# Looping over the batches and loading each adjacency unit in two halves

## The chip, the cores and the metric

The kernel runs on one core of a Trainium2 chip. The metric is the device time of one execution in microseconds. A second number, the span, is the time from the first to the last instruction in a profiled execution.

## The reference

```python
# x: (8, 2048, 64), adj (called W): (8, 2048, 2048), U: (2048, 16), w_scale: scalar, all float32
Ws = 0.5 * (W + jnp.swapaxes(W, -1, -2))
A = jax.nn.sigmoid(U @ U.T)
K = Ws * A[None, :, :]
deg = jnp.maximum(K.sum(axis=-1), EPS)
d = jax.lax.rsqrt(deg)
K = K * d[:, :, None] * d[:, None, :]
y = w_scale * jnp.einsum('bnm,bmc->bnc', K, x)
out = _layernorm(x + y, axis=-1)
```

For each of 8 batches a 2048 x 2048 matrix of 16 MB is read, made symmetric, multiplied by a gate that is the same for all batches, normalized by its row sums on both sides and applied to x. A layer norm over the 64 channels follows.

## The kernel before

Each batch's matrix is cut into 4 x 4 units of 512 x 512, 1 MB each, held in SBUF as `K[(i, j)]`, a tile of 128 partitions by 4 chunks by 512. There is one buffer for each of the 16 units, so the units of the next batch are loaded into the buffers that this batch frees. The symmetric sum and the row sums are made in ten steps (`STEPS`, pairs i >= j), of four rows each (128 matrix rows): rows 0 to 39 of a batch. The steps are (0,0), (1,0), (1,1), (2,0), (3,0), (2,1), (3,1), (3,2), (2,2), (3,3).

For one row of step (i, j) PE transposes pieces of K[(j, i)] into the PSUM ring `tw` (four banks, L394 called by `transpose_adjacency`), DVE adds them to K[(i, j)] (`add_row`, L663), then multiplies by the gate and sums the row (`gate_product`, L674, which signals `lower_done`). PE transposes the result back into the PSUM pair `kt` (L394, called by `transpose_rows`) and ACT copies it to K[(j, i)] (`upper_row`, L556, `upper_done`). When a group of rows has its degrees, POOL makes d and DVE makes z = d * x (L694). PE then forms the products z^T K (L434), in eight pairs of units (`PAIRS`): (0,0) with (0,1), (0,2) with (0,3), (1,0) with (1,1), (1,2) with (1,3), (2,0) with (2,1), (3,0) with (3,1), (2,2) with (2,3), (3,2) with (3,3). Each pair has four chunks, each of two products, and the last one signals `prod_done`. The layer norm of a batch runs on DVE, POOL and ACT two batches later.

All orders are written out by hand. A table gives for each piece of work the row at which it stands; `PRODUCT_ROWS` places the 32 product chunks of a batch at rows 29 to 65, where 40 and more mean rows of the next batch. `steps(b, lags)` issues the 40 rows of batch b with what is left of the one or two batches before; each engine has its own. The batches are unrolled by Python, so every wait is against a constant.

SP issues the loads (`load_unit`, L250). `load_pair(b, q)` waits for `prod_done` of pair q in the batch before and then loads both units of the pair, (0,1) ahead of (0,0) in pair 0, otherwise the first named first. Behind pair 5 stands the store of batch b - 2. Each unit has its own semaphore `loaded`, for which DVE (row 0 of a step, for K[(i, j)]) and PE (row 0, for K[(j, i)]) wait.

Of the kernel before, what the change touches and what calls it, by code (L numbers as in the profile page):

```python
# [13 lines left out]
P = 128  # L14
G = 4
H = P // 2
UW = G * P
# [16 lines left out]
PAIRS = PRODUCT_ORDER  # L34
# [78 lines left out]
def bass_graph_resnorm_kernel(nc, x, adj, u, w_scale, out):  # L113
# [6 lines left out]
    with ExitStack() as ctx:  # L120
# [95 lines left out]
        tw_done, sum_done, lower_done = sem("tw_done"), sem("sum_done"), sem("lower_done")  # L216
        kt_done, upper_done = sem("kt_done"), sem("upper_done")
        deg_summed, deg_ready, d_ready, z_ready = sem("deg_summed"), sem("deg_ready"), sem("d_ready"), sem("z_ready")
        prod_done, y_copied, yt_done = sem("prod_done"), sem("y_copied"), sem("yt_done")
        f_ready, y_scaled, h_ready = sem("f_ready"), sem("y_scaled"), sem("h_ready")  # L220
# [25 lines left out]
        def _(sp):  # L246
            def load_unit(b, n):
                i, j = n
                src = adj[b, i * UW:(i + 1) * UW, j * UW:(j + 1) * UW].rearrange("(g p) m -> p g m", p=P)
                sp.dma_start(K[n][:, :, :], src).then_inc(loaded[n], 16)  # L250

            sp.dma_start(u_sb, u.rearrange("(g p n) r -> p g n r", p=P, n=G)).then_inc(h_moved, 16)
            for k, n in enumerate(FIRST_LOADS):
                if k == X_AFTER:
                    sp.dma_start(xt[:, :, :], rows_of(x, 0)).then_inc(x_loaded, 16)
                if n in ((3, 2), (2, 3)):
                    sp.wait_ge(ut_done, 8)
                if n in ((2, 2), (3, 3)):
                    sp.wait_ge(uu_done, NL)
                load_unit(0, n)  # L260
            def load_pair(b, q):
                sp.wait_ge(prod_done, b * NQ + (q + 1 - NQ))
                for n in (LOADS[0:2] if q == 0 else PAIRS[q]):
                    load_unit(b, n)

# [4 lines left out]
            for q in range(NQ):  # L270
                load_pair(1, q)
            for b in range(2, B):
                for q in range(NQ):
# [13 lines left out]
        def _(pool):  # L287
# [67 lines left out]
            steps(1, 2)  # L355
            for b in range(2, B):
                steps(b, 3)
# [22 lines left out]
        def _(pe):  # L380
            def bank_free(b, g, first):
# [4 lines left out]
                elif not first:  # L386
                    last = max(n for n in range(NL) if tw_bank[n] == tw_bank[g])
                    pe.wait_ge(sum_done, b * NL + (last + 1 - NL))

            def transpose_halves(dst, at, blocks):  # L390

# [6 lines left out]
            def transpose_adjacency(b, s, r, first):  # L398

                i, j = STEPS[s]  # L400
                if r == 0:
                    pe.wait_ge(loaded[(j, i)], b * 16 + 16)
                bank_free(b, s * G + r + 1, first)
                for row in (r, r + 1):
                    g = s * G + row
# [4 lines left out]
            def transpose_rows(b, s, r, first):  # L410
# [5 lines left out]
                if not first or g:  # L416
                    pe.wait_ge(upper_done, b * NU + g)
                for row in range(r, min(r + 2, upper_rows(s))):
                    transpose_halves([kt[:, h, :] for h in range(2)], HALF_ROW * (row % 2),
# [3 lines left out]
            def product(b, q, c, first):  # L423
# [8 lines left out]
                for n, m in PAIRS[q]:  # L432
                    at = (m % 2) * C
                    t = pe.matmul(yp[at:at + C, m // 2, :], z[:, n * G + c, :], K[(n, m)][:, c, :],  # L434
                                  start=(q == first_unit[m] and c == 0), stop=(q == last_unit[m] and c == G - 1))
                if c == G - 1:
                    t.then_inc(prod_done, 1)
# [78 lines left out]
            steps(1, 2)  # L516
            for b in range(2, B):
                steps(b, 3)
# [20 lines left out]
        def _(act):  # L539
# [77 lines left out]
            steps(1, 2)  # L617
            for b in range(2, B):
                steps(b, 3)
# [25 lines left out]
        def _(dve):  # L645
# [10 lines left out]
            def add_row(b, g):  # L656
# [3 lines left out]
                if r == 0:  # L660
                    dve.wait_ge(loaded[STEPS[s]], b * 16 + 16)
                dve.wait_ge(tw_done, b * NL + (g // 2 * 2 + 2))
# [160 lines left out]
            steps(1, 2)  # L823
            for b in range(2, B):
                steps(b, 3)
# [46 lines left out]
```

## Time and profile before

| what | value |
|---|---|
| median of 3 runs | 486.77 us |
| lowest and highest | 483.96 and 487.22 us |
| the profiled execution | 483.64 us |
| its span | 481.9 us |
| mean granted clock of PE, share of full speed | 0.988 |
| HBM traffic over the span | 296 GB/s |

The profiled execution's time is 1.7 us more than its span. The engines are called PE (TensorE), DVE (VectorE), ACT (ScalarE), POOL (GpSimd) and SP (SyncE). PEld is PE's weight load, which overlaps the matmuls. Times of rows are in microseconds from the start of the span.

### The profile page before, as it was taken

The numbers are of one execution on the slowest core, as the hardware profiler recorded it, in microseconds if no ns is written. First come the engines' busy times: TensorE is split into PE (matmuls) and PEld (weight loads), VectorE is DVE, ScalarE is ACT, GpSimd is POOL, SyncE is SP. The second block draws the span as 40 slices with busy tenths as digits, with TensorE's granted clock in tenths as the row PEclk, the third lists the DMA queues.
The fourth block names the chain that finished last, engine by engine and source line by source line (L and its number), as shares of the span: only waits on it lengthen the run. The fifth ranks groups of instructions, "written<-read, shape, count | busy, mean of one in ns | idle before, by whom it ended". The sixth has DMA issues, their size and how long they took to land.

```text
span 481.9 us, 13213 instructions
## 1 busy us (share of the span) xinstructions
PE 440.4 (91%) x5318; PEld 232.3 (48%) x5318; DVE 416.6 (86%) x1154; ACT 209.4 (43%) x655; POOL 113.8 (24%) x133
## 2 busy tenths in 40 slices
PE   7887999899989999889998999899998899999893
PEld 6555544454445534554444543465445544455351
DVE  6888867899889989999879997899889998899745
ACT  3887424453245433544254442454434542554320
POOL 0000010023410334012520243103340125203343
PEclk9999999999999999999998999989999999999998
DMA  8999799959999699968999699997999889994011
GB/s 289 387 312 391 283 372 377 310 180 365 356 365 309 251 361 368 344 253 296 361 357 300 221 350 364 325 287 266 371 354 329 284 298 357 367 296 169 1 45 44
DMA packets 101420, 143.58 MB, mean 298 GB/s; under 512 B 35824, under 2 KB 35824, under 8 KB 101360
## 3 DMA queue, kind: packets, MB, share of 16 engines
q1 hardware_dynamic: 86496, 139.01, 82.0%
q10 hardware_dynamic: 14864, 3.74, 3.7%
q8 instruction: 42, 0.69, 0.6%
q14 instruction: 18, 0.15, 0.1%
HBM read 138.54 MB, written 4.19 MB: 296 GB/s over the span
## 4 chain that ended last, share of the span: by engine, by line
PE 56%; DMA 21%; DVE 13%; ACT 4%; issue 3%; SPq 2%; POOL 0%; POOLq 0%; DVEq 0%
PE yp L434 33%; DMA k<-in_adj_dram 20%; PE tw L394 9%; PE kt L394 9%; DVE k L663 5%; DVE k L674 5%; PE yp L532 3%; ACT k L556 2%; SPq L250 2%; ACT gate L543 2%; PE yp L467 1%; DVE deg L684 1%; DMA h<-in_L_gnn_U_dram 1%; PE kt L478 1%; PE kt L532 0%
## 5 line engine op out<-in xcount | busy, mean ns | idle before, releaser
L556 ACT ACTIVATE k<-kt 128x512 f32<-128x512 f32 (+3 forms) x288 | 149.5, 524 | 230.8 <-PE kt L394 230.7
L434 PE MATMUL yp<-k,z 128*64 128x512 f32 x944 | 234.9, 610 | 2.1 <-DVE z L694 2.0
L663 DVE TENSOR_TENSOR k<-tw,k 128x512 f32<-128x512 f32 (+2 forms) x320 | 193.8, 606 | 37.5 <-DMA k<-in_adj_dram 21.2
L674 DVE CUSTOM_DVE_ANT_0 k<-k,gate 128x512 f32<-128x512 f32 (+2 forms) x320 | 198.3, 620 | 0.0
L394 PEld LDWEIGHTS kt<-ident,k 64*128 64x128 f32 x1920 | 73.5, 140 | 89.6 <-DVE deg_parts L674 41.4
L394 PEld LDWEIGHTS tw<-ident,k 64*128 64x128 f32 x2176 | 81.8, 140 | 67.1 <-issue 43.3
L394 PE MATMUL kt<-ident,k 64*128 64x64 f32 x1920 | 93.0, 230 | 22.2 <-DVE deg_parts L674 14.2
L394 PE MATMUL tw<-ident,k 64*128 64x64 f32 x2176 | 99.3, 229 | 5.5 <-DMA k<-in_adj_dram 3.0
L434 PEld LDWEIGHTS yp<-k,z 128*64 128x64 f32 x944 | 55.5, 136 | 67.5 <-issue 54.8
L326 POOL TENSOR_TENSOR d<-deg,minus_half 128x4 f32<-128x4 f32 x32 | 32.5, 1015 | 216.4 <-DVE deg L684 215.7
L556 ACT ACTIVATION_READ_ACCUMULATOR k<-kt 128x1 f32 x288 | 57.2, 199 | 0.0
L308 POOL TENSOR_TENSOR h<-h,mean 128x256 f32<-128x256 f32 x28 | 17.7, 633 | 46.5 <-DVE deg_parts L674 46.5
L302 POOL TENSOR_TENSOR h<-h,x_keep 128x256 f32<-128x256 f32 x28 | 21.2, 766 | 31.0 <-DVE deg_parts L674 31.0
L319 POOL TENSOR_TENSOR h<-h,rstd 128x256 f32<-128x256 f32 x28 | 17.1, 615 | 46.1 <-DVE deg_parts L674 46.0
L674 DVE DVE_READ_ACCUMULATOR2_ANT deg_parts<- 128x1 f32 x320 | 25.9, 81 | 0.0
L314 POOL TENSOR_TENSOR rstd<-var,minus_half 128x16 f32<-128x16 f32 x7 | 21.1, 3020 | 15.4 <-DVE var L725 15.4
L543 ACT ACTIVATE gate<-yp 128x512 f32<-128x512 f32 (+3 forms) x40 | 19.9, 536 | 2.1 <-PE yp L467 1.9
L467 PE MATMUL yp<-ut_b,ut_a 128*128 128x512 f32 (+3 forms) x40 | 15.0, 432 | 1.6 <-ACT gate L543 1.5
L694 DVE TENSOR_TENSOR z<-xt,d 128x256 f32<-128x256 f32 x32 | 13.8, 432 | 2.3 <-POOL d L326 2.3
L682 DVE TENSOR_REDUCE deg<-deg_parts 128x4 f32<-128x20 f32 x32 | 5.4, 169 | 9.1 <-ACT k L556 9.1
L532 PE MATMUL yp<-k,z 128*64 128x256 f32 (+1 forms) x80 | 12.5, 467 | 0.1
L568 ACT ACTIVATE y_sb<-h 128x1024 f32<-128x1024 f32 x7 | 7.4, 1057 | 8.0 <-POOL h L308 8.0
(53 smaller groups left out, 140.1 us busy)
## 6 DMA issues: line engine op xcount, KB each, us to landing
k<-in_adj_dram SPq DMA_DIRECT2D x128, 1024.0 KB, 8.2
xt<-in_x_dram ACTq DMA_DIRECT2D x7, 512.0 KB, 8.5
out_dram<-h SPq DMA_DIRECT2D x7, 512.0 KB, 8.2
xt<-in_x_dram SPq DMA_DIRECT2D x1, 512.0 KB, 14.0
out_dram<-k SPq DMA_DIRECT2D x2, 128.0 KB, 2.1
out_dram<-k SPq DMA_DIRECT2D x3, 64.0 KB, 1.7
h<-in_L_gnn_U_dram SPq DMA_DIRECT2D x1, 128.0 KB, 3.2
out_dram<-k ACTq DMA_DIRECT2D x1, 64.0 KB, 1.9
```

What stands on the lines that cost most here:

```text
L302: nc.gpsimd.tensor_tensor(h[:, part(k), :], h[:, part(k), :], x_keep[:, part(k), :], ALU.add).then_inc(h_ready, 1)
L308: nc.gpsimd.tensor_tensor(h[:, part(k), :], h[:, part(k), :], per_row(mean, part(k).start, part(k).stop), ALU.add).then_inc(centered, 1)
L314: nc.gpsimd.tensor_tensor(rstd[:, :], var[:, :], minus_half[:, :], ALU.pow).then_inc(rstd_ready, 1)
L326: nc.gpsimd.tensor_tensor(d[:, s], deg[:, s], minus_half[:, s], ALU.pow).then_inc(d_ready, 1)
L394: t = pe.transpose(dst[h][:, at + k * H:at + (k + 1) * H], block[H * h:H * h + H, :], ident[H * h:H * h + H, H * h:H * h + H])
L434: t = pe.matmul(yp[at:at + C, m // 2, :], z[:, n * G + c, :], K[(n, m)][:, c, :], start=(q == first_unit[m] and c == 0), stop=(q == last_u ...
L467: pe.matmul(yp[:, g % 2, 0:w], ut_a[:, (i * G + r) * P:(i * G + r + 1) * P], ut_b[:, j * UW:j * UW + w], start=True, stop=True).then_inc(u ...
L532: t = pe.matmul(y, z[:, n * G + c, :], K[(n, m)][:, c, columns], start=(c0 > 0 and at == 0), stop=(at == len(chunks) - 1))
L543: nc.scalar.activation(A[:, A_AT[g]:A_AT[g] + w], yp[:, g % 2, 0:w], ACT.Sigmoid).then_inc(gate_ready, 1)
L556: nc.scalar.activation(K[(j, i)][:, r, c0:UW].rearrange("p (c h e) -> p c h e", h=2, e=H), whole_rows(kt[:, 0:2, :], r % 2, (UW - c0) // P ...
L663: nc.vector.tensor_tensor(row, whole_rows(tw[:, tw_bank[g] // 2 * 2:tw_bank[g] // 2 * 2 + 2, :], g % 2, w // P), row, ALU.add).then_inc(su ...
L674: nc.vector.tensor_tensor_reduce(row, row, A[:, A_AT[g]:A_AT[g] + w], 1.0, 0.0, ALU.mult, ALU.add, deg_parts[:, i * G + r, j:j + 1]).then_ ...
```

## The change

Three things change together. On each engine the batches 2 to 7 become one loop (`Fori`) whose body runs six times, while batches 0 and 1 and the tail stay written out. Inside the loop each wait compares with a register, which register instructions compute from the loop's counter. On PE, `settle` puts a semaphore increment behind the waits of each group of transposes, in the loop alone, so that these waits stand on that instruction and not on the first transpose. And each unit is loaded by two transfers of 512 KB: chunks 0 and 1 of both units of a pair when the pair's second product chunk is done (`half_done`), chunks 2 and 3 when its fourth is (`prod_done`). `loaded` then counts 32 for a unit, and the engines wait for both halves.

```diff
--- before.py
+++ after.py
@@ -215,7 +215,9 @@
         uu_done, gate_ready = sem("uu_done"), sem("gate_ready")
         tw_done, sum_done, lower_done = sem("tw_done"), sem("sum_done"), sem("lower_done")
         kt_done, upper_done = sem("kt_done"), sem("upper_done")
+        banks_taken = sem("banks_taken")
         deg_summed, deg_ready, d_ready, z_ready = sem("deg_summed"), sem("deg_ready"), sem("d_ready"), sem("z_ready")
+        half_done = sem("half_done")
         prod_done, y_copied, yt_done = sem("prod_done"), sem("y_copied"), sem("yt_done")
         f_ready, y_scaled, h_ready = sem("f_ready"), sem("y_scaled"), sem("h_ready")
         h_summed, mean_ready, centered, squared = sem("h_summed"), sem("mean_ready"), sem("centered"), sem("squared")
@@ -244,10 +246,11 @@
 
         @block.sync
         def _(sp):
-            def load_unit(b, n):
+            def load_half(b, n, half):
                 i, j = n
-                src = adj[b, i * UW:(i + 1) * UW, j * UW:(j + 1) * UW].rearrange("(g p) m -> p g m", p=P)
-                sp.dma_start(K[n][:, :, :], src).then_inc(loaded[n], 16)
+                r0 = i * UW + half * 2 * P
+                src = adj[b, r0:r0 + 2 * P, j * UW:(j + 1) * UW].rearrange("(g p) m -> p g m", p=P)
+                sp.dma_start(K[n][:, 2 * half:2 * half + 2, :], src).then_inc(loaded[n], 16)
 
             sp.dma_start(u_sb, u.rearrange("(g p n) r -> p g n r", p=P, n=G)).then_inc(h_moved, 16)
             for k, n in enumerate(FIRST_LOADS):
@@ -257,11 +260,13 @@
                     sp.wait_ge(ut_done, 8)
                 if n in ((2, 2), (3, 3)):
                     sp.wait_ge(uu_done, NL)
-                load_unit(0, n)
+                for half in range(2):
+                    load_half(0, n, half)
             def load_pair(b, q):
-                sp.wait_ge(prod_done, b * NQ + (q + 1 - NQ))
-                for n in (LOADS[0:2] if q == 0 else PAIRS[q]):
-                    load_unit(b, n)
+                for half, done in enumerate((half_done, prod_done)):
+                    sp.wait_ge(done, b * NQ + (q + 1 - NQ))
+                    for n in (LOADS[0:2] if q == 0 else PAIRS[q]):
+                        load_half(b, n, half)
 
             def store(b):
                 sp.wait_ge(normed, LN_PARTS * (b + 1))
@@ -269,7 +274,7 @@
 
             for q in range(NQ):
                 load_pair(1, q)
-            for b in range(2, B):
+            with sp.Fori(2, B) as b:
                 for q in range(NQ):
                     load_pair(b, q)
                     if q == STORE_PAIR:
@@ -353,7 +358,7 @@
 
             steps(0, 1)
             steps(1, 2)
-            for b in range(2, B):
+            with pool.Fori(2, B) as b:
                 steps(b, 3)
             for k in range(NZ):
                 if DEG_ROWS[k] >= NL:
@@ -387,6 +392,11 @@
                     last = max(n for n in range(NL) if tw_bank[n] == tw_bank[g])
                     pe.wait_ge(sum_done, b * NL + (last + 1 - NL))
 
+            def settle(b):
+
+                if not isinstance(b, int):
+                    pe.sem_inc(banks_taken, 1)
+
             def transpose_halves(dst, at, blocks):
 
                 for k, block in enumerate(blocks):
@@ -399,8 +409,9 @@
 
                 i, j = STEPS[s]
                 if r == 0:
-                    pe.wait_ge(loaded[(j, i)], b * 16 + 16)
+                    pe.wait_ge(loaded[(j, i)], b * 32 + 32)
                 bank_free(b, s * G + r + 1, first)
+                settle(b)
                 for row in (r, r + 1):
                     g = s * G + row
                     transpose_halves(tw_banks(g), HALF_ROW * (g % 2),
@@ -415,6 +426,7 @@
                     pe.wait_ge(lower_done, b * NL + G * (s + 1))
                 if not first or g:
                     pe.wait_ge(upper_done, b * NU + g)
+                settle(b)
                 for row in range(r, min(r + 2, upper_rows(s))):
                     transpose_halves([kt[:, h, :] for h in range(2)], HALF_ROW * (row % 2),
                                      [K[(i, j)][:, c, row * P:(row + 1) * P]
@@ -433,6 +445,8 @@
                     at = (m % 2) * C
                     t = pe.matmul(yp[at:at + C, m // 2, :], z[:, n * G + c, :], K[(n, m)][:, c, :],
                                   start=(q == first_unit[m] and c == 0), stop=(q == last_unit[m] and c == G - 1))
+                if c == G // 2 - 1:
+                    t.then_inc(half_done, 1)
                 if c == G - 1:
                     t.then_inc(prod_done, 1)
 
@@ -514,7 +528,7 @@
             transpose_u(0)
             steps(0, 1)
             steps(1, 2)
-            for b in range(2, B):
+            with pe.Fori(2, B) as b:
                 steps(b, 3)
             for row in range(NL):
                 uppers_at(B - 1, row, 1, False)
@@ -615,7 +629,7 @@
             copy_u(0)
             steps(0, 1)
             steps(1, 2)
-            for b in range(2, B):
+            with act.Fori(2, B) as b:
                 steps(b, 3)
             for row in range(NL):
                 uppers_at(B - 1, row, 1)
@@ -658,7 +672,7 @@
                 w = lower_width(s, r)
                 row = K[STEPS[s]][:, r, 0:w].rearrange("p (c h e) -> p c h e", h=2, e=H)
                 if r == 0:
-                    dve.wait_ge(loaded[STEPS[s]], b * 16 + 16)
+                    dve.wait_ge(loaded[STEPS[s]], b * 32 + 32)
                 dve.wait_ge(tw_done, b * NL + (g // 2 * 2 + 2))
                 nc.vector.tensor_tensor(row, whole_rows(tw[:, tw_bank[g] // 2 * 2:tw_bank[g] // 2 * 2 + 2, :], g % 2, w // P),
                                         row, ALU.add).then_inc(sum_done, 1)
@@ -821,7 +835,7 @@
             copy_u(0)
             steps(0, 1)
             steps(1, 2)
-            for b in range(2, B):
+            with dve.Fori(2, B) as b:
                 steps(b, 3)
             gate_product(B - 1, NL - 1, False)
             for k in range(NZ):
```

On SP the loads of one pair in the middle of the unrolled program are one wait and two transfers before:

```order
L250 DMA k<-in_adj_dram 128x4x512 [waits prod_done]
L250 DMA k<-in_adj_dram 128x4x512
L250 DMA k<-in_adj_dram 128x4x512 [waits prod_done]
L250 DMA k<-in_adj_dram 128x4x512
L250 DMA k<-in_adj_dram 128x4x512 [waits prod_done]
L250 DMA k<-in_adj_dram 128x4x512
```

After the change, in the loop, there are four transfers, with waits for `half_done` and `prod_done`, and instructions that set registers (ISA and REGISTER_ALU) between them:

```order
L253 ISA [waits half_done]
L253 DMA k<-in_adj_dram 128x2x512
L253 ISA
L253 DMA k<-in_adj_dram 128x2x512
L253 ISA [waits prod_done]
L253 DMA k<-in_adj_dram 128x2x512
L253 ISA
L253 DMA k<-in_adj_dram 128x2x512
L267 REGISTER_ALU
```

A pair's first halves now stand ahead of the wait for its last products, and the second half of the first unit stands behind the first half of the second.

On PE, before, at the boundary between the rows of two batches: the last products and back transposes, then the first transposes of the next batch, which wait for the unit (0,0) (`loaded_00`):

```order
L434 MATMUL yp<-k,z 64x512 [waits z_ready]
L434 MATMUL yp<-k,z 64x512 x3
L394 MATMUL kt<-ident,k 128x64 [waits upper_done,lower_done]
L394 MATMUL kt<-ident,k 128x64 x9
L434 MATMUL yp<-k,z 64x512 x4
L394 MATMUL tw<-ident,k 128x64 [waits sum_done,loaded_00]
L394 MATMUL tw<-ident,k 128x64 x5
L394 MATMUL kt<-ident,k 128x64 [waits upper_done]
L394 MATMUL kt<-ident,k 128x64
L394 MATMUL tw<-ident,k 128x64 [waits sum_done]
L394 MATMUL tw<-ident,k 128x64 x13
```

After, the end of the loop's body:

```order
L439 REGISTER_ALU
L446 MATMUL yp<-k,z 64x512 [waits z_ready]
L446 MATMUL yp<-k,z 64x512 x3
L428 REGISTER_ALU [waits lower_done]
L404 MATMUL kt<-ident,k 128x64 [waits upper_done]
L404 MATMUL kt<-ident,k 128x64 x9
L446 MATMUL yp<-k,z 64x512 x4
L531 REGISTER_ALU
L531 COMPARE_AND_BRANCH
```

and its head, to which the branch goes back:

```order
L531 ISA
L393 ISA [waits loaded_00]
L404 MATMUL tw<-ident,k 128x64 [waits sum_done]
L404 MATMUL tw<-ident,k 128x64 x5
L428 ISA
L404 MATMUL kt<-ident,k 128x64 [waits upper_done]
L404 MATMUL kt<-ident,k 128x64
L404 MATMUL tw<-ident,k 128x64 [waits sum_done]
L404 MATMUL tw<-ident,k 128x64 x13
```

The same matmuls stand in the same order; a branch lies between the products and the transposes, and a register instruction ahead of most groups. The semaphore instructions of `settle` are not printed in these lists; they stand ahead of each group of transposes and hold the last wait that is shown on it. PE's loop body has 584 matmul instructions of the program (648 matmuls and as many weight loads on the engine), 41 register instructions, 8 fused ones and 40 semaphore instructions. DVE's body has 203 instructions, of them 47 register instructions and 12 fused ones.

On DVE the head of the loop's body, which before held no register instructions:

```order
L838 ISA
L676 ISA [waits loaded_00]
L677 TENSOR_TENSOR k<-tw,k 128x128 [waits tw_done]
L687 ISA
L688 ISA k,deg_parts<-k,gate 128x512 [waits sum_done]
L688 ISA deg_parts 128x1
L694 REGISTER_ALU
L695 ISA [waits lower_done]
```

Each operation waits for the same semaphores as before, now with a register instruction ahead of some.

## Rows read from the trace of the kernel before

**Rows 1.** The page: busy time by engine, and the chain's shares by engine.

```profile
PE 440.4 (91%) x5318; PEld 232.3 (48%) x5318; DVE 416.6 (86%) x1154; ACT 209.4 (43%) x655; POOL 113.8 (24%) x133
...
PE 56%; DMA 21%; DVE 13%; ACT 4%; issue 3%; SPq 2%; POOL 0%; POOLq 0%; DVEq 0%
```

**Rows 2.** Windows, one batch: busy us (x instructions), PEclk, DMA share, GB/s.

```profile
155.00:210.00 55.00, 52.74 (x664) 27.23 (x660) 50.37 (x141) 23.62 (x77) 15.05 (x18) 1.00 0.94 326
```

**Rows 3.** Waits, 100 to 435: who waited for whom, us, times, longest.

```profile
PEld kt L394 <- DVE deg_parts L674: 31.9, 34, 1.9
...
DVE k L663 <- DMA k<-in_adj_dram: 16.4, 17, 2.4
...
PE kt L394 <- DVE deg_parts L674: 11.9, 15, 1.7
...
PE tw L394 <- DMA k<-in_adj_dram: 2.7, 3, 1.3
PE tw L394 <- DVE k L663: 2.1, 10, 0.2
```

**Rows 4.** Timeline of DVE, 155 to 210: the three waits for a load.

```profile
179.47 0.69 DVE L663 TENSOR_TENSOR k<-tw,k 128x512 f32<-128x512 f32 x1 [0.27 <-DMA k<-in_adj_dram]
...
190.79 0.69 DVE L663 TENSOR_TENSOR k<-tw,k 128x512 f32<-128x512 f32 x1 [0.70 <-DMA k<-in_adj_dram]
...
196.95 0.69 DVE L663 TENSOR_TENSOR k<-tw,k 128x512 f32<-128x512 f32 x1 [1.19 <-DMA k<-in_adj_dram]
```

**Rows 5.** Windows of 2 us at a batch's start.

```profile
159.00:161.00 2.00, 2.00 (x36) 1.31 (x32) 2.00 (x7) 1.15 (x4) 1.24 (x2) 1.00 0.18 62
161.00:163.00 2.00, 2.00 (x24) 0.92 (x22) 2.00 (x6) 0.37 (x3) 0.91 (x2) 1.00 0.00 0
163.00:165.00 2.00, 2.00 (x24) 0.78 (x22) 1.97 (x9) 1.01 (x4) 0.14 (x1) 1.00 0.81 239
165.00:167.00 2.00, 2.00 (x30) 1.01 (x26) 2.00 (x8) 1.27 (x4) 1.70 (x2) 1.00 1.05 410
```

**Rows 6.** Timeline, 156 to 163: pair 0's products, and the loads behind them.

```profile
156.68 1.94 PE L434 MATMUL yp<-k,z 128*64 128x512 f32 x8
...
160.12 1.94 PE L434 MATMUL yp<-k,z 128*64 128x512 f32 x8
...
162.10 0.92 SPq L250 DMA_DIRECT2D k<-in_adj_dram  x2
```

**Rows 7.** Timeline, 191.9 to 192.9: what two late groups of transposes waited for.

```profile
192.01 0.08 DVE L674 DVE_READ_ACCUMULATOR2_ANT deg_parts<- 128x1 f32 x1
192.01 0.69 DVE L663 TENSOR_TENSOR k<-tw,k 128x512 f32<-128x512 f32 x1
...
192.14 0.53 PE L394 MATMUL kt<-ident,k 64*128 64x64 f32 x10
...
192.84 0.28 PE L394 MATMUL tw<-ident,k 64*128 64x64 f32 x2 [0.17 <-DVE k L663]
```

**Rows 8.** Timeline of PE, 187.5 to 192.9: groups that were not late.

```profile
187.65 0.71 PE L394 MATMUL kt<-ident,k 64*128 64x64 f32 x16
188.19 0.67 PE L394 MATMUL tw<-ident,k 64*128 64x64 f32 x16
...
189.81 0.72 PE L394 MATMUL kt<-ident,k 64*128 64x64 f32 x16
190.35 0.67 PE L394 MATMUL tw<-ident,k 64*128 64x64 f32 x16
```

**Rows 9.** DMA queues: packets, MB, share of 16 engines.

```profile
q8 instruction: 42, 0.69, 0.6%
```

**Rows 10.** Page, DMA issues: KB each, us to landing.

```profile
h<-in_L_gnn_U_dram SPq DMA_DIRECT2D x1, 128.0 KB, 3.2
```

**Rows 11.** Timeline of PE, 155 to 208, at the end of a batch's rows.

```profile
170.60 0.53 PE L394 MATMUL kt<-ident,k 64*128 64x64 f32 x10
171.06 1.94 PE L434 MATMUL yp<-k,z 128*64 128x512 f32 x8
```

## The prediction

> **What bounds the kernel now.** I read the page first: TensorE is busy 91% of the span, VectorE 86%, and the chain that ended last is 56% TensorE, 21% DMA and 13% VectorE [rows 1]. No engine stands alone, so I cut the span by batch. A batch takes some 55 us; in 155 to 210 us PE is busy 52.74 us, DVE 50.37, and the DMA engines 94% [rows 2]. PE therefore idles some 2.3 us of a batch, and that is all that a better supply of data can give back there.
>
> The waits say what the idle time is. From 100 to 435 us (335 us, six batches) VectorE stood 16.4 us in L663 for an adjacency unit, in 17 waits; in 155 to 210 these are three, of 0.27, 0.70 and 1.19 us, 2.16 together [rows 3, 4]. They fall, by the order of the steps, on (1,0), (2,0) and (3,0), each the first unit of its pair; call these A units and the second ones B. TensorE's own waits mostly follow from them: kt for `lower_done`, 11.9 us in 15 waits, and tw for `sum_done`, 2.1 us in 10 [rows 3].
>
> Why units are late: a batch's first load goes out at 162.10, when the second half of pair 0's products (started at 160.12) has ended. In 159 to 163 us the DMA engines are busy 0.18 and 0.00 of the time, in 163 to 165 0.81; summed, 1.64 + 2.00 + 0.38, about 4.0 us idle. Behind that the stream runs at 410 GB/s [rows 5, 6], and over the batch the engines are busy 94% [rows 2], so what is lost here is late for the rest of the batch.
>
> **Part 1, half transfers.** The first half of pair 0 is free when the 8 matmuls that began at 156.68 end, 158.6, against 162.1 now: 3.5 us sooner [rows 6]. In that time two transfers of 512 KB go, 1 MB. At 400 GB/s this is 2.6 us, moved into the 4.0 us of idle DMA, so everything behind it may land up to 2.6 us sooner. But the order within a pair changes: now A whole, B whole; then A's first half, B's first half, A's second, B's second. A is complete after 1.5 MB of the pair, not after 1 MB, which is 1.3 us later. So B gains 2.6 us, A gains 1.3 us. The waits are `b * 32 + 32`, for the whole unit, so no row can start on half of one. The waits that cost are on the A units, so I take 1.3 us a batch of the 2.16 [rows 4], in each of seven batches (1 to 7): **-9 us**. The bounds: 0 if A's delay eats the lead; and from the top -20 us, the 16.4 us of six batches and as much again as one average batch for batch 1, and a little of PE's own waits for DMA, 2.7 us [rows 3]. I stay low because a unit that comes sooner leaves PE with at most 2.3 us a batch.
>
> SP issues 16 more transfers a batch, each 0.4 to 0.5 us: the two at 162.10 take 0.92 [rows 6]. That is 16 x 0.46 = 7 us of SP in 55, which are covered by the time that SP now spends waiting. I cost it at nothing; without that cover it would be 7 us a batch. The store of batch b-2 still stands ahead of pair 6 on SP; its wait for `normed` now also holds back pair 6's first half, which puts it where it was.
>
> The Trainium skill speaks against this part: the page "DMA: Bandwidth & Descriptors" gives a fixed part of about 2 us for each transfer (Anatomy of one DMA) and the rule to batch transfers to 1 MiB or more (Bandwidth). Here the trace shows two loads that are issued in 0.92 us as one row and a stream of 410 GB/s right behind it, so that the fixed part of one lies under the bytes of another [rows 5, 6]; by the page, were it not hidden, each unit would pay one fixed part more, 16 of 2 us a batch, and the kernel would be far slower. What a weaker form of it does is the third rival.
>
> **Part 2, waits on registers in the loop.** In the loop PE's waits for `sum_done` and `upper_done` no longer stand on the transposes but on a semaphore instruction ahead of them (`settle`). Rows show both kinds in the kernel before. kt at 192.14, whose last wait (`lower_done`) is on the matmul, starts 0.05 us after the VectorE row at 192.01 (0.08 long) has ended. tw at 192.84, whose late wait (`sum_done`) is on a semaphore instruction, as it also waits for `loaded`, starts 0.14 us after the L663 row of 192.01 (0.69 long) [rows 7]. So a late wait costs **0.09 us** more when a semaphore instruction holds it. Where nothing is late it costs nothing: tw at 188.19 has such an instruction (it also waits for `loaded_02`), tw at 190.35 has none, and both start 0.54 us after the kt before [rows 8]. The array really stood idle for such a wait 28 times in 100 to 435 (15 + 10 + 3) [rows 3]: 28 x 0.09 = 2.5, **+3 us** for the six batches of the loop. The bounds are 0 (they lie beside DVE's time) and +6 us, if weight loads are counted, which stopped about twice as often as the array (kt for DVE 34 times for 15).
>
> That an instruction of the sequencer alone holds back everything behind it while it waits, and an engine's own instruction waits in a queue, is also what the Trainium skill says ("Perfetto Trace Analysis", Per-engine timelines). It has no price for it; 0.09 us is the rows'.
>
> The values of those registers are computed by 41 register instructions and 8 fused ones in PE's loop body, 47 and 12 in DVE's. No row shows one. They stand ahead of the waits, so where PE waits they are hidden, and behind products the sequencer has 1 us of matmuls to hide them under. The lower bound is 0; the upper is that each costs what a semaphore instruction costs at worst, 0.09 us: 49 x 6 x 0.09 = 26 us. I take a fifth of it, **+5 us**, since the nearest row, the satisfied semaphore instruction, is at 0. DVE's are covered by operations of 0.5 to 0.7 us each; ACT and POOL idle most of a batch [rows 1].
>
> **Part 3, the back edge.** Five of them are taken. The trace before shows straight code being fetched: 42 packets, 0.69 MB in all, for PE (5318 matmuls and as many weight loads [rows 1], 253 a packet) [rows 9]. What a jump back costs no row shows. If the head is still on the engine it is next to nothing. If it must be fetched, the nearest row is a small transfer, 3.2 us to land 128 KB [rows 10]. Part of that is covered: PE has 10 transposes and 8 matmuls behind the last held wait (170.60 to 173.00, 2.4 us) [rows 11], so 0 to 0.8 us show. VectorE has one addition and one gate product behind its last wait, 0.69 + 0.68 + 0.08 = 1.45 us as at 192.01 [rows 7], and 0.3 to 1.8 us show. I take half of the largest, 0.9 us, five times: **+4.5 us**; the bounds are 0 and 5 x 3.2 = 16 us.
>
> The Trainium skill has two statements on it ("Runtime: NRT & Kernel Launch", Instruction fetch mechanics): an instruction memory of 2048 instructions for PE and 512 for the others, and that a taken branch whose target isn't in a window of two pages forces a fetch. By the first, PE's body of about 1,390 and DVE's of 203 fit and the edge is free; by the second, PE pays each time. No run here shows which holds; the second is rival 2.
>
> **The sum.** -9 + 3 + 5 + 4.5 = +3.5 us on the profiled execution's 483.64: 487.1. That execution is 3.1 us below the median of the runs, 486.77, which go from 483.96 to 487.22. I put half of this difference on top, since neither can be told from the other as the level: **489 us**, in a range of its own from 482 to 497.
>
> **Rivals.** (1) *The loop is free, the loads pay.* Terms of part 2 and 3 come to 2 us, the lead gives 9 to 16: 483.6 - 9 + 2 = 477 to 470, with the same half of 3.1 on top 471 to 478. For it: a satisfied semaphore instruction costs nothing [rows 8], 4 us of idle DMA in each batch [rows 5]. Against: PE has only 2.3 us a batch to give back. (2) *Each back edge is a stall in the open*, the other side: PE and DVE both refetch, while the 16 DMA engines are 94% busy, and nothing of the 3.2 us is covered because the register waits keep the sequencers from running ahead. 483.6 - 9 + 3 + 5 + 16 = 498.6, about 500. It decides from some 2.4 us an edge, where PE's cover ends. (3) *The halves bring nothing*: A units come no sooner or 512 KB transfers run a few per cent slower; with the loop's 12.5 us that is 496 to 498. The wait for half a unit doesn't exist in VectorE, which speaks for it; the idle DMA stretch speaks against it.
>
> **Chances.** My forecast 0.45, rival 1 0.28, rival 2 0.17, rival 3 0.10. The range that holds 8 in 10 reaches from 473 to 503. A measurement of this kernel can tell about 1% from no change, that is 481.9 to 491.6. Rival 1 and a small piece of mine (0.02) are faster, 0.30; of mine 0.30 lie within 1%; the rest of mine (0.13) and rivals 2 and 3 are slower, 0.40.
>
> **What would show it.** In the profile after: DMA idle at a batch's start near 1.4 us for 4.0; VectorE's waits on adjacency loads in L677 near 7 us for six batches instead of 16.4; TensorE's idle time ahead of transposes up by 0.1 us a group; a gap on PE or DVE at five points about 55 us apart; instruction packets still counted at five times a batch's worth if heads are refetched, fewer if they stay. I am wrong if register instructions cost more than 0.02 us each on PE, if the loads' order within a pair decides the late waits, or if the edge is above 1 us.

## The result, and the profile of the changed kernel

The changed kernel takes 493.19 us (median of 4 runs, 490.06 to 495.16), the kernel before beside it 487.0 us: a ratio of **1.0158, interval 1.0101 to 1.0216**. In a second series, of 12 runs, it is 490.41 us and 1.0118 (1.0082 to 1.0154). So it is slower by 1.2 to 1.6 per cent, 6 to 8 us. Every ratio here is formed over fast runs alone, without those over 1.5% above the kernel's fastest, and differs by up to half a per cent from the quotient of two medians (here 1.0127). The forecast was 489 us. The experiments show that this total was nearly right by terms that were not.

The page of the changed kernel: engines, the queues of the loads (q1) and of the instructions (q8), the chain, and the loads' time to landing.

```profile
PE 446.5 (91%) x5318; PEld 236.0 (48%) x5318; DVE 418.6 (85%) x1154; ACT 209.5 (43%) x655; POOL 113.5 (23%) x133
...
q1 hardware_dynamic: 88544, 139.02, 84.8%
...
q8 instruction: 17, 0.28, 0.2%
...
PE 52%; DMA 23%; DVE 11%; issue 8%; ACT 3%; POOL 0%; SPq 0%; DVEq 0%; POOLq 0%
...
k<-in_adj_dram SPq DMA_DIRECT2D x256, 512.0 KB, 7.4
```

Beside [rows 1] DMA has a larger share of the chain, 23% for 21%, and "issue" has risen, 8% for 3%. The instruction packets have fallen from 42 [rows 9] to 17: the loops save 25 of them.

The waits of the changed kernel, 100 to 435 us, the groups that answer to [rows 3]:

```profile
DVE k L677 <- DMA k<-in_adj_dram: 22.4, 23, 2.7
PE kt L404 <- DVE deg_parts L688: 16.7, 22, 2.0
...
PE tw L404 <- DMA k<-in_adj_dram: 2.0, 4, 0.8
...
PE kt L404 <- issue: 1.6, 2, 1.4
PE tw L404 <- DVE k L677: 1.5, 9, 0.2
```

The loads come later, not sooner: VectorE waits 22.4 us for them (19.1 in the traced execution of the second series), where it was 16.4 and I expected 7. The 1.4 us of "issue" is one gap, which the run on TensorE's increments explains. Windows of 2 us at the start of the same batch as in [rows 5]:

```profile
163.00:165.00 2.00, 1.97 (x22) 1.09 (x24) 0.66 (x3) 1.23 (x4) 0.00 (x0) 1.00 0.90 329
165.00:167.00 2.00, 1.66 (x33) 1.02 (x31) 1.95 (x5) 0.04 (x1) 0.49 (x1) 1.00 0.11 31
167.00:169.00 2.00, 2.00 (x24) 0.84 (x20) 2.00 (x5) 1.26 (x4) 1.36 (x3) 1.00 0.86 278
169.00:171.00 2.00, 2.00 (x24) 1.06 (x24) 2.00 (x6) 0.95 (x3) 0.30 (x1) 1.00 0.88 259
171.00:173.00 2.00, 2.00 (x38) 1.13 (x34) 1.97 (x11) 0.31 (x2) 0.75 (x1) 1.00 1.07 299
173.00:175.00 2.00, 2.00 (x16) 0.62 (x16) 1.93 (x7) 1.27 (x4) 1.10 (x2) 1.00 0.93 216
```

The last two columns, the DMA engines' busy share and GB/s, carry the reading. From 163 to 171 us the DMA engines idle 0.20 + 1.78 + 0.28 + 0.24 = 2.5 us, for 4.0 before: the earlier start is there. But the stream behind it, with the engines 86 to 107% busy, runs at 216 to 299 GB/s, where [rows 5] show 410. Two windows side by side overstate this, and this batch starts slowest of the seven. By the trace's DMA records, bytes over busy time in the 10 us behind a batch's first load are 283 to 328 GB/s in batches 1 to 7, for 334 to 358 before; over 65 to 430 us they are 335 for 353. The lead comes with slower transfers.

### The profile page after: what moved, and what is told of

Read it like the earlier page. It is cut to its first block, busy times and chain, and to the rows that moved or that the text cites. A ratio compares the mean times of both kernels' runs of the same rounds, so it can differ in the third digit from the quotient of the medians.

```text
span 492.8 us, 14768 instructions
## 1 busy us (share of the span) xinstructions
PE 446.5 (91%) x5318; PEld 236.0 (48%) x5318; DVE 418.6 (85%) x1154; ACT 209.5 (43%) x655; POOL 113.5 (23%) x133
## 4 chain that ended last, share of the span: by engine, by line
PE 52%; DMA 23%; DVE 11%; issue 8%; ACT 3%; POOL 0%; SPq 0%; DVEq 0%; POOLq 0%
PE yp L446 29%; DMA k<-in_adj_dram 23%; PE kt L404 10%; PE tw L404 8%; DVE k L677 6%; PE yp L546 3%; DVE k L688 2%; ACT k L570 2%; PE yp L481 2%; ACT gate L557 1%; DVE deg_parts L688 1%; DVE var L736 1%; PE kt L492 1%; PE kt L546 0%; SPq L253 0%
## 5 line engine op out<-in xcount | busy, mean ns | idle before, releaser
L688 DVE CUSTOM_DVE_ANT_0 k<-k,gate 128x512 f32<-128x512 f32 (+2 forms) x320 | 200.8, 628 | 0.0
L404 PEld LDWEIGHTS kt<-ident,k 64*128 64x128 f32 x1920 | 74.9, 141 | 95.7 <-issue 78.0
L404 PE MATMUL kt<-ident,k 64*128 64x64 f32 x1920 | 94.1, 231 | 27.7 <-DVE deg_parts L688 19.7
L404 PEld LDWEIGHTS tw<-ident,k 64*128 64x128 f32 x2176 | 83.0, 141 | 67.5 <-issue 62.0
L404 PE MATMUL tw<-ident,k 64*128 64x64 f32 x2176 | 101.0, 230 | 6.1 <-DMA k<-in_adj_dram 3.5
L481 PE MATMUL yp<-ut_b,ut_a 128*128 128x512 f32 (+3 forms) x40 | 17.3, 493 | 1.5 <-ACT gate L557 1.3
L546 PE MATMUL yp<-k,z 128*64 128x256 f32 (+1 forms) x80 | 12.5, 467 | 0.1
```

What stands on the lines that cost most here:

```text
L404: t = pe.transpose(dst[h][:, at + k * H:at + (k + 1) * H], block[H * h:H * h + H, :], ident[H * h:H * h + H, H * h:H * h + H])
L481: pe.matmul(yp[:, g % 2, 0:w], ut_a[:, (i * G + r) * P:(i * G + r + 1) * P], ut_b[:, j * UW:j * UW + w], start=True, stop=True).then_inc(u ...
L546: t = pe.matmul(y, z[:, n * G + c, :], K[(n, m)][:, c, columns], start=(c0 > 0 and at == 0), stop=(at == len(chunks) - 1))
L688: nc.vector.tensor_tensor_reduce(row, row, A[:, A_AT[g]:A_AT[g] + w], 1.0, 0.0, ALU.mult, ALU.add, deg_parts[:, i * G + r, j:j + 1]).then_ ...
```

## The experiments

All ratios are to the kernel before on the same chip. Diffs are against the kernel that is named.

**The changed kernel again, and each part alone.** Halves alone: the changed kernel with every `Fori` written out (which also drops `settle`'s increments). Loops alone: the changed kernel with 1-MB units.

```diff
# halves alone, on each of the five engines
-            with pe.Fori(2, B) as b:
+            for b in range(2, B):
# loops alone
-                for half, done in enumerate((half_done, prod_done)):
-                    sp.wait_ge(done, b * NQ + (q + 1 - NQ))
-                    for n in (LOADS[0:2] if q == 0 else PAIRS[q]):
-                        load_half(b, n, half)
+                sp.wait_ge(prod_done, b * NQ + (q + 1 - NQ))
+                for n in (LOADS[0:2] if q == 0 else PAIRS[q]):
+                    load_unit(b, n)
```

> The changed kernel once more, on the chip that runs the next three, so that they share its runs of the kernel before. Expected 1.016 of the kernel before, within 1.010 to 1.022.

> Half transfers alone: the batches are unrolled again, all waits are against constants, and settle does nothing. Theory D (the transfers cost the time, the loop is free): 490 to 494 us, ratio 1.01 to 1.02, and the DMA queue's busy time near 418 us as in the changed kernel, against 395 before. Theory L (the loop costs, the halves are worth what the prediction says): 475 to 482 us, ratio 0.98 to 0.99.

> The loops alone: units are loaded by one transfer of 1 MB behind prod_done as before. Theory D: 485 to 488 us, ratio 0.997 to 1.003. Theory L: 493 to 500 us, ratio above 1.012; the prediction's terms of 3, 5 and 4.5 us would give 1.025.

Measured: halves alone **0.9924** (0.9885 to 0.9963), loops alone **0.9826** (0.9752 to 0.9901), both together 1.0118. Neither theory holds: each part gains by itself, and together they lose. The two parts cannot be costed apart.

**The size of a transfer, without the earlier start.** All four 512-KB transfers of a pair wait for `prod_done` and go unit after unit, first written out, then in the loops.

```diff
-                for half, done in enumerate((half_done, prod_done)):
-                    sp.wait_ge(done, b * NQ + (q + 1 - NQ))
-                    for n in (LOADS[0:2] if q == 0 else PAIRS[q]):
+                sp.wait_ge(prod_done, b * NQ + (q + 1 - NQ))
+                for n in (LOADS[0:2] if q == 0 else PAIRS[q]):
+                    for half in range(2):
                         load_half(b, n, half)
```

> Unrolled, two transfers of 512 KB for each unit, but all four of a pair behind prod_done and one unit after the other: the size alone, with no early half and no other order. If each transfer has a fixed share of the DMA engines' time (22.8 us for 128 more in the changed kernel, 0.18 us each), the queue's busy time is 418 us here too and the ratio 1.01 to 1.02, as nothing is won. If it is the early halves that break up the stream (transfers that start on an empty queue), the busy time is near 395 us and the ratio within 0.5% of 1.

> The changed kernel with its loops, but a pair's four 512-KB transfers all wait for the whole pair's matmuls and go unit after unit, as in the size-only run, which had no loops. Theory S (a transfer has a price of its own, and the loops take their 1.7 per cent off whatever the transfers are): the size-only run's 1.029 times the loops' 0.983, so 1.01. Theory X (halves and loops disturb each other on SP, where a loop's register instructions put the four transfers of a pair 0.56 us apart instead of 0.41): above 1.025, and packets of over 1 us in the loop. If the order of the halves is what matters and the loop is neutral to it, the changed kernel (1.012) and this one differ as the two unrolled kernels do, by 3.6 per cent, and this one is at 1.05.

Measured: 1.0289 (1.0236 to 1.0341) written out and 1.0298 (1.0241 to 1.0354) in the loops. Cutting a unit in two costs 2.9%, 14 us, when nothing starts sooner (some 2 us of it may be a lower granted clock, 0.977 for 0.984 written out; in the loops the clock is no lower). Written out, the loads' queue is busy 80.4% of 502.5 us, 404 us, between the 395 and the 418 of the two expectations, and the time is above both. Set against halves alone, the earlier start by chunk, with its order A, B, A, B, is worth 1.0289 less 0.9924, 3.6%, or 18 us. The loops, worth 1.7% with 1-MB units, are worth nothing here. The number is the one that I gave to spacing on SP, but the written-out kernel loses as much, so it speaks for the size and not for the loops.

**TensorE's increments alone.** The kernel before with constant waits, and `settle` from batch 1 on.

```diff
+            def settle(b):
+                if b >= 1:
+                    pe.sem_inc(banks_taken, 1)
```

> The kernel before, unrolled, with 1-MB units and constant waits; only TensorE's extra semaphore increment ahead of each group of transposes is added, from batch 1 on, so that a late wait is held by that instruction. The prediction's term: 28 late waits times 0.09 us in a batch, +3 us in all, ratio 1.006. Rival: the instruction passes while TensorE has queued matmuls, and costs nothing: 1.000, within 0.3 per cent. Second rival: it keeps the next weight load from going ahead under the matmuls at each of the 56 groups of a batch, not the late ones alone, 0.09 us each: +35 us, ratio 1.07.

Measured: **1.0158** (1.0116 to 1.0199), +7.7 us on 486.5, above the term and far below the second rival. (The term's 28 late waits are those of six batches, not of one, as I wrote.) The trace shows two things. The first is the one predicted: a kt group that is late starts 0.15 us after the end of the gate product it waited for, where it is 0.06 in the kernel before (medians over 18 such groups in each, 65 to 430 us). 18 x 0.09 = 1.6 us. The second I had not thought of. TensorE's timeline, 262 to 270 us:

```profile
265.59 0.65 PE L400 MATMUL tw<-ident,k 64*128 64x64 f32 x14
269.22 0.37 PE L400 MATMUL tw<-ident,k 64*128 64x64 f32 x2 [2.99 <-issue]
```

and the DMA queues of this kernel in 266.0 to 269.3 us:

```profile
q8 instruction: 1, 0.02, 2.0%
```

Fourteen of sixteen transposes are done, nothing is waited for, and the last two come 2.99 us later; one packet of instructions went through in that time (its record starts at 266.86 and takes 1.05 us). There are four such gaps of over 0.5 us between 100 and 435 us, of 0.65, 1.20, 2.99 and 1.40 us, 6.2 together, and a fifth of 2.05 us at 445.31. Before each, an instruction packet's record ends 1.3 to 1.7 us ahead of TensorE's next matmul. The kernel before has as many packets, 42 for 43, and no such gap. So I read: the increment keeps the sequencer from running ahead, and a fetch that used to pass unseen comes into the open. No run took the fetches away and left the code written out. The sum is 1.6 + 8.3 = 9.9 us, of the 13.5 by which this execution's span (495.4 us) exceeds the one before; the runs' ratio makes 7.7. Some 2 us may be the clock: the granted clock of this kernel's runs is 0.973 on average, that of the kernel before beside them 0.982, and among the runs of the latter 0.01 of clock goes with 2 to 3 us. (For the other ratios here, but the size-only run's above, the clock makes about a microsecond or less.)

In the loops the same increments have nothing to expose once the body has run through. In its first pass there is one such gap in six of the seven traces with TensorE's loop, of 0.8 to 1.4 us; in the changed kernel it is 1.42 us, up to 160.93, and a packet's record ends 1.4 us ahead of that. Behind it there is none. The DMA queues of the changed kernel in 175 to 460 us, all of the rows:

```profile
q1 hardware_dynamic: 52752, 84.41, 89.0%
q10 hardware_dynamic: 10320, 2.62, 4.0%
q14 instruction: 1, 0.01, 0.0%
```

No packet on q8 at all, where the kernel before has 26 in that stretch.

**Spacing on SP.** Halves alone, with two increments that nobody waits for ahead of each transfer.

```diff
                     for n in (LOADS[0:2] if q == 0 else PAIRS[q]):
+                        for _ in range(2):
+                            sp.sem_inc(filler, 1)
                         load_half(b, n, half)
```

> Halves alone, unrolled (0.992 in the first call), with two semaphore increments that nobody waits for ahead of every transfer on SP: they space a pair's transfers as the loop's register instructions do. Theory X (the halves lose inside the loop because SP issues them later and farther apart): most of the step from 0.992 to 1.012 comes back, ratio 1.005 or more. Theory S (spacing on SP costs nothing; the changed kernel loses elsewhere): within 0.4 per cent of 0.992.

Measured: **0.9994** (0.9959 to 1.0029), 0.7% above halves alone, which ran on another chip, and between the two theories. By the trace two transfers of a pair follow each other after 0.56 us instead of 0.44 (means of 94), and in the changed kernel, where SP computes registers between them, after 0.57. So spacing can be a part of the loss, and not all of it.

**Only pair 0 in halves, in the loops.** The stretch with idle DMA engines is at the batch's start, so this should have kept the lead and paid for two more transfers a batch.

```diff
-                for half, done in enumerate((half_done, prod_done)):
+                if q == 0:
+                    sp.wait_ge(half_done, b)
+                    for n in LOADS[0:2]:
+                        load_half(b, n, 0)
+                sp.wait_ge(prod_done, b * NQ + (q + 1 - NQ))
+                # then second halves for pair 0, load_unit for the others
```

> The changed kernel with its loops, but only the two units of pair 0 go by halves (their first halves after half of that pair's matmuls); all other units are single 1-MB transfers. The stretch that had idle DMA queues is the one at the batch's start, so if what the halves give is the earlier start there, this keeps it and pays for 2 extra transfers a batch instead of 16. Expected by that: the loop-alone kernel's 0.983 less some 1.3 us a batch, 0.965 to 0.98. If the halves give nothing at the batch's start and the wait only moves to the next pair of units: 0.983 or a little above. If the halves of pair 0 are what disturbs the loop: 1.00 or above.

Measured: 0.9973 (0.9937 to 1.0009). A miss: with two more transfers a batch the loops' gain is nearly gone, 1.5% above the loops alone, which ran on another chip. VectorE's waits for loads are about the same, 8.9 us for 9.7 in the loops alone, but its waits for TensorE's tw rise from 8.8 to 13.1, and TensorE's for the gate product from 8.4 to 12.5 (100 to 435 us). I can't say why from the rows.

**Which engine's loop.** With 1-MB units and with halves, TensorE alone written out (constants, no increments) or alone looping.

```diff
# "loops but PE", from the loops alone and from the changed kernel
-            with pe.Fori(2, B) as b:
+            for b in range(2, B):
# "PE only": the same on sp, pool, act and dve instead
```

> The loops-alone kernel (1-MB units, 0.983) with TensorE's program written out again, with constants and without its extra semaphore increments; the other four engines loop. Theory F (the loops gain because the written-out programs are fetched through the same DMA engines, 25 of the 33 fewer fetch packets being TensorE's): TensorE's fetches are back, so most of the gain is gone: 0.99 to 1.00, and 42 packets on the larger instruction queue. Theory R (the gain comes from the other engines' loops, and TensorE's register waits with their increments, 1.016 by themselves, eat into it): 0.983 less 0.016, 0.967.

> The reverse: 1-MB units, TensorE alone loops, with its increments and register waits; the other four engines are written out. Theory F: 25 of the 33 saved packets stay saved: 0.983 to 0.99, 17 packets on the larger instruction queue. Theory R: only the cost of TensorE's increments and waits stays: 1.016 or above.

> The changed kernel with TensorE's program written out again, with constants and without its increments; SP and the others loop, units go by halves. Additive account (halves 0.992, wider spacing on SP +0.007, TensorE's increments gone): 0.999, within 0.5 per cent. If the halves' loss inside the loops comes from TensorE's increments and register waits alone: 0.992 or below. If it comes from the loops of the other engines, SP's above all: 1.01, as the changed kernel.

> The changed kernel with its transfers by halves and TensorE's loop (with its increments), the other four engines written out: the one corner still missing of halves by TensorE's loop by the other loops. If the three parts act by themselves (halves 0.992, TensorE's loop 0.992, other loops 1.006), 0.984, and the changed kernel's 1.012 to 1.016 comes only from all three together. If halves and TensorE's loop disturb each other (halves with the other loops are 1.004, the changed kernel 1.012 to 1.016, so about +0.010 for TensorE's loop where it gives 0.008 with 1-MB units): 1.002, and the transfers' share of the DMA engines is near the changed kernel's (84.7 per cent of its span) rather than the 83.5 of halves alone.

All eight corners, ratios to the kernel before:

| | PE written out | PE loops |
|---|---|---|
| 1-MB units, the others written out | 1 | 0.992 (0.9885 to 0.9954) |
| 1-MB units, the others loop | 1.0065 (1.0023 to 1.0106) | 0.983 (0.9752 to 0.9901) |
| halves, the others written out | 0.992 (0.9885 to 0.9963) | 1.0077 (1.004 to 1.0113) |
| halves, the others loop | 1.0036 (0.9989 to 1.0083) | 1.0118 and 1.0158 |

With 1-MB units TensorE's loop gains, though it carries the increments. With halves it costs 1.5%. **The change loses by this pairing**, and it does so without the other engines' loops already: 1.0077, where 0.992 x 0.992 would be 0.984, and above the 1.002 that I had put on a disturbance. The other engines' loops cost 0.65% and 1.1% where TensorE is written out, near the 0.7% of the spacing run; that spacing on SP is the cost with 1-MB units too was not run. Where TensorE loops they seem to gain with 1-MB units (0.992 to 0.983, the intervals touch). With halves the additive account's 0.999, within 0.5%, held: 1.0036. Theory R is out: TensorE's loop is the part that gains. Theory F predicted the sides rightly, with 17 and 42 packets, but both of its ranges were too low, 0.99 to 1.00 for 1.0065 and 0.983 to 0.99 for 0.992.

What the pairing does to the loads shows in their queue. One row each, 65 to 430 us (packets, MB, share of the 16 engines): PE alone looping with 1-MB units, then halves alone, then halves with TensorE's loop.

```profile
q1 hardware_dynamic: 68416, 114.44, 88.3%
```

```profile
q1 hardware_dynamic: 69771, 113.78, 90.0%
```

```profile
q1 hardware_dynamic: 69722, 113.68, 93.0%
```

MB divided by share times 365 us is the speed while the engines are busy: 355, 346 and 335 GB/s. Over all kernels, one traced execution each, this sorts cleanly:

| kernels | GB/s while busy |
|---|---|
| 1-MB units: before, TensorE's increments alone, three with loops | 353, 354, 353, 355, 355 |
| pair 0 in halves, all loop | 349 |
| halves, PE written out: alone, with filler, others loop | 346, 346, 347 |
| size only: written out, in the loops | 346, 343 |
| halves by chunk with PE's loop: other engines written out; the changed kernel twice | 335, 337, 335 |

In the changed kernel the same bytes keep the engines busy 353/335, 5% longer. It isn't the clock, which was 0.974 and 0.993 in its two traced executions (335 and 337 GB/s). But that the slower transfers are what costs the time is not shown. The traced execution of halves with TensorE's loop, the fastest of its 12, took 484.15 us at 335 GB/s, and that of halves alone 484.01 us at 346; the loops alone and the kernel before move 353 both, and the loops are 1.7% faster.

## Why the prediction came out as it did

The total, 489 for 490 to 493 us, was right and so was the side; the account was not. The forecast had the halves gain 9 us and the loops cost 12.5. Alone the halves gain 3.7 and the loops gain 8.4, and what makes the whole slower is a term that the forecast didn't have. That the total came out is luck. By its own steps:

**Halves, -9 us.** Mechanism half right. The lead exists, 1.5 us less idle time at the batch's start in the windows for the 2.6 that I moved there (by the DMA records, from 6 us before a batch's first load to 12 us behind it, 0.9 us less a batch over batches 2 to 7). Alone the halves gained 0.76%, 3.7 us, and VectorE's waits for loads fell only from 16.4 to 15.1 us. The step that failed is "a stream of 410 GB/s right behind it, so that the fixed part of one lies under the bytes of another": cut transfers stream 2% slower, 346 for 353 GB/s, which over some 49 us of stream in a batch (87.8% of the time in 65 to 430 us) is 1 us, most of the 1.3 us that I counted; by the DMA records the 10 us behind a batch's first load are slower in halves alone too, 313 to 343 GB/s. That I read two 1-MB loads issued together as evidence for 512-KB ones was the mistake; those rows say nothing of size. The rule of the Trainium skill on size ("DMA: Bandwidth & Descriptors", Bandwidth), which I set aside, pointed the right way, and the size-only run's 2.9% agrees with it, though it is far from a fixed part paid in full for each unit. (The fixed part stands in that page's section on transfers issued from GpSimd; these are issued from SP.)

**Waits held by an increment, +3 us.** The price of one was right where waits are constants, 0.09 us; in the loop it is double for the wait for `lower_done`. The order list of the loop has that wait on a register instruction, ahead of the increment; a late wait for `upper_done`, which stands on the increment, costs 0.09 in the loop too. VectorE and TensorE of the changed kernel at 166 us:

```profile
166.26 0.08 DVE L688 DVE_READ_ACCUMULATOR2_ANT deg_parts<- 128x1 f32 x1
...
166.59 0.40 PE L404 MATMUL kt<-ident,k 64*128 64x64 f32 x6 [0.34 <-DVE deg_parts L688]
```

166.59 - 166.34 = 0.25 us, where [rows 7] show 0.05. Over the 24 late kt groups of the loop the median is 0.24, so 24 x 0.18 = 4.3 us for 3. Late tw groups start 0.15 us after their release in both kernels. What I left out is that the same increment can lay a fetch bare, 8 us in the unrolled kernel and 1.4 in the first pass of the loop.

**Register instructions, +5 us.** Too high. What the rows show is that further 0.09 us in the late kt groups, some 2 us, already counted in the 4.3, and 0.08 us in one to four late product groups of a kernel. On VectorE, which I held to be covered, they do show: of its late waits in 175 to 430 us those for loads end 0.11 us after the landing for 0.02 before, in 18 waits, and those for tw 0.02 us after for 0.09, in 12, 0.8 us in all. On SP, where I costed everything at nothing, they do cost: 0.13 us more between the transfers of a pair, worth 0.7% by the filler run, if registers cost what increments cost there. The idle time of SP, by which I had costed its work at nothing, was beside the point: how late a transfer goes out counts, not SP's load.

**The back edge, +4.5 us.** It is free. TensorE jumps between the products and the six tw transposes of this timeline of the changed kernel:

```profile
179.70 0.60 PE L446 MATMUL yp<-k,z 128*64 128x512 f32 x2
180.23 0.40 PE L404 MATMUL tw<-ident,k 64*128 64x64 f32 x6
180.46 0.23 PE L404 MATMUL kt<-ident,k 64*128 64x64 f32 x2
```

There is no gap; 237.47 and 293.89 look the same. VectorE's edge is free too: its first addition of a pass waits 0.64 us for tw at all five, and 0.64 us before (173.44 and 229.32). Of the two statements of the Trainium skill ("Runtime: NRT & Kernel Launch", Instruction fetch mechanics) the trace bears out the first, a body that stays in memory: no packet for TensorE from 175 to 460 us. Rival 2, built on the second, is out. Beyond being free, the loop saves what the fetches cost, which I had put at nothing: with 1-MB units TensorE's loop alone is 2.4% below the unrolled kernel that has the same increments, from a batch earlier (0.992 and 1.016), 11.5 us. In the traced execution of the latter the five gaps make 8.3 us, and some 2 may be the clock. The rest may be the loads: of the 16 engines' shares of a 1-MB unit the last lands 1.52 us after the first in the kernel before, 1.63 where the others loop, 1.11 with TensorE's loop and 0.73 in the loops alone (means of 96 units, from the trace's DMA records), and a fetch packet holds one of the 16 engines some 1.05 us. That this spread is the gain is argued, not shown; no run added fetches to a loop.

**The sum.** -4 for the halves and -8 for the loops would be -12. What made it +6 to +8 is that the parts act on each other: 0.9924 x 0.9826 would be 0.975, and 1.012 to 1.016 was measured, 18 to 20 us that no step contained. 11 of them are the pairing of halves and TensorE's loop (1.0077 for 0.984). Rival 3 named slower transfers, but for the halves alone. None of my three signs of being wrong named a meeting of the parts. I added terms that were each read from rows of unlooped 1-MB code, and much of the cost lies in their meeting.

## What to carry to other kernels

Time two parts of a change separately and together before trusting the sum: here 0.992 and 0.983 made 1.012. If code is unrolled, look at the instruction queue's packets: here a loop removed 25 of 42, and a semaphore instruction ahead of each group went with gaps of 0.65 to 2.99 us behind five of them. To see whether smaller transfers are free, divide the bytes by the DMA share over a steady stretch, and then time them: idle time at a batch's start is only half of the question, and a lower speed need not cost time. The loops with whole units (480.86 us, for 485.5 of the kernel before beside it) are the version to keep.

## What the runs showed of the hardware that was not expected

A loop of some 1,390 instructions on TensorE ran six times with no packet on its instruction queue from 175 to 460 us. An unrolled TensorE's fetches left no gap over 0.5 us without held waits; with them there were gaps of 0.65 to 2.99 us behind five of 43. 512-KB transfers moved 346 GB/s while busy and 1-MB ones 353 to 355, and only with TensorE looping did those by chunk fall to 335 to 337. Why TensorE's program should slow the loads' packets is open: its fetches are gone there, so it isn't their traffic. By the trace's records the lengthened packets come mostly 28 to 32 us into a batch and in its last 12 us, counted from the last gate product of the batch before, and I have no row that names what they wait for.
